# A 96-byte unused tile ahead of the feed-forward weight factors in SBUF

## The reference

```
emb = silu(sin_emb(timestep)) @ W_ada + b_ada
scale, shift = split(emb)
x = ln(src) * (1 + scale) + shift
q, k, v = x @ Wq + bq, x @ Wk + bk, x @ Wv + bv
probs = softmax(where(mask, -inf, q @ k.T / sqrt(32) + attention_bias))
x = x + (probs @ v) @ Wo + bo
h = ln(x) * g2 + beta2
out = x + gelu2(h @ W1 + b1) @ W2 + b2          # gelu2(z) = z * sigmoid(1.702 z)
```

## Time and profile before

| | us |
|---|---|
| median of 3 runs | 2446.56 |
| lowest, highest | 2445.44, 2448.83 |
| span of the profiled execution | 2446.8 |
| TensorE (PE) busy | 2363.3 (97%) |
| weight loads (PEld) busy | 2225.6 (91%) |
| GpSimd (POOL) busy | 1833.0 (75%) |
| VectorE (DVE) busy | 1740.3 (71%) |
| ScalarE (ACT) busy | 1323.8 (54%) |

### The profile page before, as it was taken

How to read it: one execution, slowest core, us unless ns; L and a number is a source line. 1 busy time by engine, 2 the same in 40 slices (tenths; PEclk the granted TensorE clock), 3 DMA queues, 4 the chain that set the end, 5 groups by cost and what they waited for, 6 DMA issues and landing times.

```text
span 2446.8 us, 61264 instructions
## 1 busy us (share of the span) xinstructions
PE 2363.3 (97%) x21034; PEld 2225.6 (91%) x21034; DVE 1740.3 (71%) x2864; ACT 1323.8 (54%) x3663; POOL 1833.0 (75%) x1787
## 2 busy tenths in 40 slices
PE   5999999999999999978999999999979999999998
PEld 3888888888888888868999999999979999999998
DVE  5777777777777777676666667675577677676766
ACT  2666666666666666665555555555443334333432
POOL 3777777777777777778777777777897676767775
PEclk9999999999999999999999999999999999999999
DMA  7344444444444444323434343433465555656563
GB/s 241 115 131 139 136 141 140 139 128 126 134 136 140 141 140 145 101 92 118 164 135 162 146 152 146 152 146 147 164 207 174 188 188 181 190 171 192 173 195 125
DMA packets 289442, 372.13 MB, mean 152 GB/s; under 512 B 29072, under 2 KB 203280, under 8 KB 289232
## 3 DMA queue, kind: packets, MB, share of 16 engines
q1 hardware_dynamic: 289232, 369.44, 46.4%
HBM read 251.68 MB, written 117.70 MB: 151 GB/s over the span
## 4 chain that ended last, share of the span: by engine, by line
PE 90%; POOL 3%; DVE 3%; issue 2%; DMA 1%; ACT 1%; SPq 0%; DVEq 0%; POOLq 0%; ACTq 0%
PE up L1601 14%; PE up L1599 14%; PE up L1600 14%; PE psD L956 5%; PE turn L956 5%; PE psD L958 5%; PE psD L957 5%; PE turn L958 5%; PE turn L957 5%; PE psS L985 4%; PE psS L971 3%; PE psC L995 3%; PE turn L1599 2%; PE turn L1600 2%; PE turn L1601 2%
## 5 line engine op out<-in xcount | busy, mean ns | idle before, releaser
L1599 PE MATMUL up<-T,wc 128*128 128x256 f32 x1792 | 512.3, 286 | 14.1 <-DVE gu L1473 7.8
L1601 PE MATMUL up<-T,wc 128*128 128x256 f32 x1792 | 508.5, 284 | 0.0
L1600 PE MATMUL up<-T,wc 128*128 128x256 f32 x1792 | 506.1, 282 | 0.0
L628 POOL TENSOR_TENSOR s<-s,rinv 128x512 f32<-128x512 f32 x254 | 265.0, 1044 | 221.6 <-DVE rinv L823 221.5
L744 ACT ACTIVATE s<-s,nmx 128x128 f32<-128x128 f32 x1024 | 396.2, 394 | 7.4 <-issue 4.3
L1599 PE MATMUL up<-wc,gs 128*128 128x256 f32 x1280 | 360.9, 282 | 2.3 <-DVE gs L1556 2.3
L1600 PE MATMUL up<-wc,gs 128*128 128x256 f32 x1280 | 360.5, 282 | 0.0
L1601 PE MATMUL up<-wc,gs 128*128 128x256 f32 x1280 | 360.4, 282 | 0.0
L1599 PEld LDWEIGHTS up<-T,wc 128*128 128x128 f32 x1792 | 340.1, 190 | 17.9 <-DVE gu L1473 9.0
L688 POOL TENSOR_TENSOR bias<-bias,mneg 128x512 f32<-128x512 f32 x256 | 335.5, 1334 | 11.2 <-DVE mneg L828 11.2
L1600 PEld LDWEIGHTS up<-T,wc 128*128 128x128 f32 x1792 | 341.6, 191 | 0.0
(11 more groups left out here) (221 smaller groups left out, 6964.6 us busy)
## 6 DMA issues: line engine op xcount, KB each, us to landing
bias<-in_bias SPq DMA_DIRECT2D x128, 512.0 KB, 5.4
gated<-gu SPq DMA_DIRECT2D x128, 512.0 KB, 2.6
adab<-ada_rows SPq DMA_DIRECT2D x64, 512.0 KB, 5.4
gbuf<-gated SPq DMA_DIRECT2D x64, 512.0 KB, 3.9
gu<-gated SPq DMA_DIRECT2D x63, 512.0 KB, 3.8
xin<-in_x SPq DMA_DIRECT2D x32, 512.0 KB, 5.0
resid<-rout SPq DMA_DIRECT2D x64, 256.0 KB, 2.0
r<-resid SPq DMA_DIRECT2D x16, 1024.0 KB, 6.1
```

The costliest lines, as they stand in the source:

```text
L628: eng.tensor_tensor(s[:, b, heads, :], s[:, b, heads, :], rinv[:, b, heads].unsqueeze(2).to_broadcast([P, HG, S]), ALU.mult).then_inc(done, 1)
L1599: pe.matmul(out_ap, sh, mh, start=start, stop=False)
L1600: pe.matmul(out_ap, sh, ml, start=False, stop=False)
L1601: return pe.matmul(out_ap, sl, mh, start=False, stop=stop)
```

## The change

One tile of 24 float32 (96 bytes in each partition) is placed ahead of `wc`, and nothing writes or reads it. `wc` moves from byte 95,264 to 95,360, `gu` from 209,952 to 210,048, `s1p` from 226,336 to 226,432; all three then are multiples of 128 bytes, and 128 modulo 512, as T0, T1, gs0 and gs1 are. No other tile moves. No instruction, no order and no wait changes on any engine: the lists of instructions of the two programs are the same, row for row; only addresses differ.

```
-        wc, gu, s1p = at_once(("wc", [P, 8, 2, 7, 2 * P], F32R), ("gu", [P, 4, 4, 2 * P], F32), ("s1p", [P, 2, 2 * P], F32))
+        ahead, wc, gu, s1p = at_once(("ahead_wc", [P, 24], F32), ("wc", [P, 8, 2, 7, 2 * P], F32R), ("gu", [P, 4, 4, 2 * P], F32), ("s1p", [P, 2, 2 * P], F32))
```

## The result

The changed kernel takes 2459.74 us (median of 4 runs, 2456.54 to 2460.54) against 2446.0 for the kernel before (median of 4 runs, 2442.91 to 2448.83). The forecast was 2406. The case that had the direction right is the third, with a chance of 0.17; its own sum, 2534, was far too large.

The account below looks back on a forecast made before the run. TensorE's matmul stream was taken as the bound. Gains of 24.2 us in `up` and 16.7 in `down`, with nothing from other engines, made 40.9 off 2446.8, forecast 2406 us, range 2379 to 2460.

Parts of the forecast that it names:

- the third: Rival for `up` and `down`: operands starting equal modulo 512 disturb each other; slower, 2452 to 2534 us; chance 0.17.
- What bounds the kernel: TensorE's stream, busy 97% of the span; matmul intervals of 120.0 ns in `up` and 118.6 in `down`, 1282.7 us together.
- Users other than TensorE: VectorE's reads of `gu` and the loads into it, in `down`: gain nothing, as `gu` and gbuf differ by 1%.
- TensorE: the step that failed: Matmuls of `up` and `down`: with aligned operands, 115.5 ns each like the projections, a gain of 40.9 us.
- The bounds of that step: `up` and `down` at the projections' lower pace, 113.0 ns, gain 67.7 us; at the higher, 118.0 ns, 14.0 us.
- Addresses modulo 128 do nothing: Rival for `up` and `down`: the pace has another cause, time stays at 2446.6 us (2442 to 2451); chance 0.36.
- rule on lines of 16 bytes: SBUF reads: only staying within a line counts; both places of `wc` start one, so zero gain and 2446.6 us.
- Even over whole stretches: Argument from `up` and `down`: a chance pace should sometimes be 113 ns, yet theirs is even over 200 us.
- Equal residues collide: Load and stream in `up` and `down` reading like places: 127.4 ns each, 87.1 us lost, 2534 us; chance 0.17.
- The range: Whole kernel: 2379 to 2460 us, taking the first two cases whole and the weakest part of the slower one.
- main case: Aligned operands in `up` and `down` run like the projections, 113.0 to 118.0 ns: 2379 to 2433 us; chance 0.46.

Follow-up runs that it names:

- e11: Kernel before with 288 unused bytes ahead of `wc`, putting it at 64 modulo 128 and 320 modulo 512; 0.9863, median 2417.18 us.
- e7: Kernel before with 96 unused bytes between `wc` and `gu`, so only `gu` and `s1p` move, to 0 modulo 128; 1.0008.
- e4: Kernel before with 96 unused bytes ahead of all tiles, so everything moves and the distances between operands stay; 1.000.
- e2: Kernel before with 32 unused bytes ahead of `wc`, putting `wc`, `gu` and `s1p` at 64 modulo 128 and modulo 512; 0.9882, median 2416.87 us.
- e10: Kernel before with 160 unused bytes ahead of `wc`, putting it at 64 modulo 128 and 192 modulo 512; 0.9944.
- e1: Kernel before run again with no edit; 0.9994, median 2448.08 us over 12 runs.
- e12: Kernel before with 32 unused bytes ahead of `wc`, a repeat of e2 for a second trace; 0.9895.
- e9: Kernel before with 224 unused bytes ahead of `wc`, putting it at 0 modulo 128 but 256 modulo 512; 1.0002, median 2449.86 us.
- e5: The changed kernel run again with no edit, against the kernel before; 1.0051.
- e6: Changed kernel with `gu` and `s1p` put back to 32 modulo 128, so `wc` alone stays moved, against the kernel before; 1.004.
- e8: Kernel before with 64 unused bytes ahead of `wc`, putting it at 96 modulo 128; 0.9953.

## Why the prediction was wrong

*What bounds the kernel* was right. TensorE stays busy for 200 of 200 us in both stretches, and the lengths of `up` and `down` follow the interval between matmuls in every trace. The loss and e11's gain came with no change in TensorE's idle time (83.5 us before, 82.7 after, 83.5 in e11).

*Users other than TensorE: nothing.* Right in what it came to, though the earlier trace rows leave GpSimd 47 and 54 us of the 200, not "60 us and more". Times of single operations do shift in the profile after: VectorE's multiplications from `gu` and gbuf, for the earlier trace rows, are

```profile
L1556 DVE TENSOR_TENSOR gs<-gu,gs 128x768 fp32r<-128x768 f32 x63 | 87.8, 1393 | 86.2 <-ACT gs L1432 86.2
...
L1556 DVE TENSOR_TENSOR gs<-gbuf,gs 128x768 fp32r<-128x768 f32 x64 | 82.6, 1291 | 107.6 <-ACT gs L1432 107.6
```

but gbuf, whose mean falls from 1360 to 1291 ns, has not moved, and e7 shows that moving `gu` and `s1p` alone is worth 1.0008 [0.9995, 1.0022].

*TensorE: the step that failed* is "the feed-forward part is the one place where float32r matmuls have an operand off a multiple of 64", and what was drawn from it: that aligned operands run like the projections. The rows of the step were read correctly, but residues of the single operands were compared where the residue of their difference counts. The projections have 64 and 0, a distance of 64; the change makes 128 and 128, a distance of 0, which is in no row. The two placements are alike in being multiples of 64 and unlike in what matters. e4 shows it from one side (`wc` aligned, distance kept: 1.000), e2 from the other (distance 64: 0.9882). With `wc` put where xT lies the reasoning by likeness to the projections comes true: e11 has 117.8 and 113.4 ns, a mean of 115.6, where the step used 115.5 for both, and takes 2417.18 us. That the mean fits is luck: e10, at the same distance modulo 128, has 117.3 and 117.8.

*The bounds of that step*, 67.7 and 14.0 us of gain, took the two paces of the projections as the two ends for any aligned pair, and so excluded a loss within this cause. `up` gained 0.0 ns and `down` lost 1.4 against the first trace (2.6 against e1), 7 to 14 us by 5376 matmuls.

*Addresses modulo 128 do nothing.* Wrong: the places of `wc` in e2 and in the changed kernel are 64 bytes apart, and the ratios 0.9882 and 1.0045. The Trainium skill's rule on lines of 16 bytes (SBUF — State Buffer, "Door 1: The DMA port swizzle"), beside which this rival stood, does not decide here: all these places of `wc` are starts of such lines, and `down` goes at 113.4 to 120.0 ns. But the argument against this rival was wrong too. A stream does fall into one pace or another at the same addresses (e1 against the earlier trace rows, e2's and e12's clusters, the projections in one execution); which paces are open to it depends on the addresses. "Even over whole stretches" showed a pace that holds for hundreds of us, not one that is fixed.

*Equal residues collide.* Right in direction and in what it compares, the two operands' starts: the distance is 0, and that is the slowest placement of those tried. That load and stream "read like places at the same time" is not shown. The mis-sized term is its price. It took the output projection's excess of 20.7 ns in 512 columns, 7.4 and 8.8 ns more per matmul; measured are 0.0 and 1.4 to 2.6. That row could not price a collision: its operands are 64 apart modulo 128, not equal. `up` could lose nothing since it was already at 120. In the traces at distance 32 the intervals of `up` run through six unequal values, from 116 to 125 ns, that repeat every 0.72 us, and at distance 0 all are 120: the same mean by another way. The argument against it, that load and stream differ in length and don't stay in step, does not hold against the runs: the distance counts, and at distance 0 the intervals are an even 120 ns.

*The range* reached to 2460 and so just holds 2459.74, by the weak end of the third case. That is luck, not the main case.

## What to carry to other kernels

When two operands stream into TensorE together, compare the distance between their starts modulo 128, not the alignment of each: the distance that was best here was 64, and equal starts were the slowest. A distance of 128 (e9) had nearly the same intervals, though not the longer time. These are differences of 0.4 to 1.4% of one kernel's time, with float32r matmuls of 256 columns and a weight load for each. Before borrowing a pace from another stage of the profile, check that the stage is alike in what the change will set; one row with the new distance would have been needed, and there was none. And a difference of some 5 us between two traces of a stage that the change does not touch can be scatter: run the kernel before a second time with a profile and see whether it repeats itself.

## What the runs showed of the hardware

The interval of a float32r matmul of 256 columns with its own weight load takes several settled values at full granted clock: 113.3, 117.8 and 120.0 ns are seen flat, all above the 106.7 that its columns cost at half clock's one column per cycle. The distance between the operands, modulo 128, sets which are open: 120.0 at 0 (119.6 to 119.9 on average where it is 128), 117.8 or 113.3 at 64, and means between 116.8 and 119.9 at 32 and 96.

Which open one is taken is a state that lasts. It changed within an execution in the attention part (from 113 to 118 ns at about 300 us in e1 to e5 and e11, between 415 and 450 in e6, e7, e12 and the changed kernel, at about 550 in e8, not at all in the first trace, e9 and e10) and stayed so until near the part's end. It is worth up to 8 us there (1032.5 to 1040.6), and 7 in `down` (e1 against the first trace); together that is near the spread of the kernel before, 2439.79 to 2454.55 us in e1, though it was not matched run by run. What picks the pace was not found.

The Trainium skill, TensorE: Matmul & The Clock Gate, "Step-by-step: what each phase is for", says that the weight load reads through a port of its own and takes nothing from the running matmul. The runs do not show which part of the two meets, only that the pair is slower or faster with their distance, 120.0 against 113.3 ns; a load without a stream beside it was not tried, and neither was moving T and gs with `wc` in its place.
